# Another order of five engines' work in a cross-attention and six-layer kernel

## The reference

```python
qkv = x @ Wqkv                      # 128 -> 3 * 1024, 16 heads of 64
q = l2norm(q) * qs                  # per head
k = l2norm(k) * ksc
q = q * cos * scale + rotate_half(q) * sin * scale
k = k * cos * inv + rotate_half(k) * sin * inv
sim = einsum(q, k) * QK_SCALE       # windows of 32 queries, 64 keys, band mask
attn = softmax(sim); out = einsum(attn, v)
out @ Wo
...
xn = (x - mu) / sqrt(var + 1e-05) * g + bln
a, gate = split(xn @ W1 + b1)       # 128 -> 2 * 341
a * gelu(gate) @ W2 + b2
```

## Time and profile before

| | |
|---|---|
| median of 3 runs | 1734.22 us (1728.39 to 1739.47) |
| the profiled execution | 1738.27 us, span 1736.5 us |
| mean granted TensorE clock | 0.967 |
| PE busy | 1532.5 us, 88% |
| PEld busy | 1223.3 us, 70% |
| DVE busy | 1360.1 us, 78% |
| ACT busy | 1244.8 us, 72% |
| POOL busy | 1264.0 us, 73% |

### The profile page before, as it was taken

One profiled execution on the slowest core, in us unless ns is written; L12 is line 12 of the kernel. 1 busy time (PEld: TensorE's weight loads), 2 busy tenths in 40 slices (PEclk: granted clock), 3 DMA queues, 4 the chain that ended last, 5 costly groups with the idle time before them and its releaser, 6 DMA issues.

```text
span 1736.5 us, 67874 instructions
## 1 busy us (share of the span) xinstructions
PE 1532.5 (88%) x28560; PEld 1223.3 (70%) x28656; DVE 1360.1 (78%) x2564; ACT 1244.8 (72%) x4601; POOL 1264.0 (73%) x1492
## 2 busy tenths in 40 slices
PE   6589989899998899999889998989999989989985
PEld 5367777677777677777667777767777767777774
DVE  4678888878887977877878787787788787887873
ACT  3267868777877777777777777786776777776773
POOL 2378787777877867867767768787778687887770
PEclk8699999999999999999999999999999999999998
DMA  4012211021211111211111212111211112111011
GB/s 120 1 40 57 57 40 52 27 58 33 67 57 35 45 47 45 67 45 47 33 28 57 67 38 60 33 40 46 57 51 47 47 33 57 27 49 45 27 45 31
DMA packets 50878, 80.62 MB, mean 46 GB/s; under 512 B 8947, under 2 KB 16806, under 8 KB 50574
## 3 DMA queue, kind: packets, MB, share of 16 engines
q1 hardware_dynamic: 50574, 76.28, 15.8%
HBM read 18.62 MB, written 1.05 MB: 11 GB/s over the span
## 4 chain that ended last, share of the span: by engine, by line
PE 63%; ACT 12%; DVE 11%; issue 7%; POOL 7%; DMA 0%; SPq 0%; POOLq 0%; DVEq 0%
PE ps L442 9%; PE ps L389 7%; PE ps L396 7%; ACT pr L650 7%; PE ps L412 6%; PE ps L452 6%; PE ps L391 5%; PE ps L390 5%; PE ps L423 4%; PE ps L483 4%; DVE v L956 2%; ACT sq L613 2%; PE ps L406 2%; POOL t L779 2%; POOL t L798 2%
## 5 line engine op out<-in xcount | busy, mean ns | idle before, releaser
L779 POOL TENSOR_TENSOR t<-t 128x512 f32<-128x512 f32 x384 | 486.2, 1279 | 84.2 <-DVE t L951 83.6
L650 ACT ACTIVATE pr<-ps,nmax 128x64 f32<-128x64 f32 x1536 | 460.6, 353 | 0.9 <-DVE nmax L966 0.9
L798 POOL TENSOR_TENSOR t<-t,rn 128x512 f32<-128x512 f32 x384 | 397.6, 1056 | 7.5
L650 ACT ACTIVATION_READ_ACCUMULATOR pr<-ps,nmax 128x1 f32 x1536 | 376.8, 248 | 0.0
L949 DVE TENSOR_TENSOR t<-ps,rope 128x512 f32<-128x512 f32 x384 | 261.6, 681 | 58.1 <-PE ps L396 37.9
L809 POOL TENSOR_TENSOR pr<-pr,rsum 128x512 f32<-128x512 f32 x192 | 200.8, 1046 | 135.1 <-DVE rsum L973 134.4
L389 PE MATMUL ps<-w_hi,xt_hi 128*128 128x512 f32 x576 | 272.7, 473 | 26.7 <-DVE t L951 10.3
L613 ACT ACTIVATE sq<-ps 128x512 f32<-128x512 f32 x384 | 233.3, 622 | 69.9 <-PE ps L391 63.2
L951 DVE TENSOR_TENSOR t<-ps,rope 128x512 f32<-128x512 f32 x384 | 260.7, 679 | 0.0
L931 DVE TENSOR_REDUCE ss<-sq 128x8 f32<-128x512 f32 x384 | 259.2, 675 | 0.7
L390 PE MATMUL ps<-w_lo,xt_hi 128*128 128x512 f32 x576 | 235.0, 408 | 3.0 <-issue 3.0
(11 more groups left out here) (122 smaller groups left out, 2714.0 us busy)
## 6 DMA issues: line engine op xcount, KB each, us to landing
v_win<-v SPq DMA_DIRECT2D x384, 128.0 KB, 2.3
wqkv<-wqkv_in SPq DMA_DIRECT2D x36, 256.0 KB, 3.9
xsh<-xr SPq DMA_DIRECT2D x24, 224.0 KB, 2.6
wo<-wo_in SPq DMA_DIRECT2D x6, 512.0 KB, 3.8
w<-w_in SPq DMA_DIRECT2D x6, 342.0 KB, 4.6
w<-w_in SPq DMA_DIRECT2D x6, 172.5 KB
x<-x_in SPq DMA_DIRECT2D x4, 256.0 KB, 4.1
out<-x SPq DMA_DIRECT2D x4, 256.0 KB, 2.7
```

Of the source, the lines that this page charges most:

```text
L650: i = A(pr[:, c, odd * SPAN:(odd + 1) * SPAN], ps[:, S_BANK[odd], c * SPAN:(c + 1) * SPAN], ACT.Exp, bias=nmax[:, odd, c:c + 1], accum_out ...
L779: G.tensor_tensor(t1[:, c, :], t1[:, c, :], t2[:, c, :], ALU.add).then_inc(qk_added[c], 1)
L798: G.tensor_tensor(w, w, rn[:, par(u), h2, a, :].unsqueeze(2).broadcast_to([P, 8, E]), ALU.mult).then_inc(done, 1)
```

## The change

The reordering touches every engine's `step(s)`; no computation is added or removed. TensorE's scores now stand between the two transposes of the probabilities, and the values come after projections Q0 and V1 of the following step, so there is other work between both. FFN gates 1 and 2 and value 0 move to the end of the step of gate 0, and `ffn_transpose` moves a step forward. `copy_o` of half 0 moves from VectorE to ScalarE. Twelve entries of the bank tables are set anew, waits are added or dropped as the order needs, the w1 splits come earlier, and `LAST_STEP` is 103. The diff, with its repeated waits on banks cut:

```diff
-    QKV_BANK = [1, 1, 0, 0, 0, 1]
-    TQ_BANK = [5, 4, 4, 5]
+    QKV_BANK = [1, 1, 0, 0, 0, 0]
+    TQ_BANK = [5, 5, 4, 5]
     TP_BANK = [4, 5]
-    GATE_BANK = [0, 1, 0]
-    VALUE_BANK = [1, 0, 1]
+    GATE_BANK = [1, 0, 1]
+    VALUE_BANK = [0, 1, 0]
     O_BANK = [6, 7]
-    Y_BANK, D_BANK, X_BANK, XH_BANK = 6, 7, 6, 5
+    Y_BANK, D_BANK, X_BANK, XH_BANK = 7, 6, 7, 4
-    FIRST_STEP, LAST_STEP = -7, 102
+    FIRST_STEP, LAST_STEP = -7, 103
```

SyncE:

```diff
-                run_layer(s, -4, load_w1, 1)
+                run_layer(s, -5, load_w1, 1)
...
+                run_quad(s, 6, shift_tokens)
                 run(s, 1, shift_v, 1)
-                run_quad(s, 6, shift_tokens)
                 run_layer(s, 2, load_wo, 1)
-                run(s, 0, shift_v, 0)
+                run(s, 1, shift_v, 0)
```

ScalarE, `step(s)` after:

```diff
+                run(s, 1, square, K1)
+                run(s, 1, upper_w, K1)
+                run_quad(s, 9, ffn_gate, 0)
+                run(s, 3, copy_pT, 0)
+                run_input(s, 10, copy_xt)
+                run_quad(s, 9, ffn_gate, 1)
+                run_quad(s, 9, ffn_gate, 2)
+                run(s, 1, guess_norm)
+                run_quad(s, 8, ffn_upper)
+                run(s, 3, copy_pT, 1)
                 run(s, 0, square, Q0)
                 run(s, 0, upper_w, Q0)
+                run(s, 2, exps, 0)
+                run(s, 3, copy_o, 0)
+                run(s, 3, copy_o, 1)
                 run(s, 1, copy_qk, Q0)
+                run(s, 2, exps, 1)
                 run(s, 1, copy_qk, K0)
                 run(s, 0, square, K0)
                 run(s, 0, upper_w, K0)
+                run(s, 1, upper_w, V1)
+                run(s, 1, copy_qk, Q1)
+                run(s, 1, upper_w, V0)
+                run(s, 0, square, Q1)
+                run(s, 0, upper_w, Q1)
+                run(s, 2, exps, 2)
+                run(s, 2, exps, 3)
+                run(s, 1, copy_qk, K1)
```

GpSimd, `step(s)` after:

```diff
+                run(s, 1, normalise_q, 1)
+                run(s, 1, normalise_k, 0)
+                run_quad(s, 7, ffn_power)
+                run(s, 1, rotate, K1)
                 run(s, 1, lower_w, K1)
+                run(s, 1, lower_w, V1)
+                run(s, 1, normalise_k, 1)
+                run(s, 2, normalise_p, 0)
+                run(s, 0, rotate, Q0)
+                run(s, 0, rotate, K0)
+                run(s, 0, lower_w, K0)
+                run(s, 2, normalise_p, 1)
+                run_layer(s, 4, split_w1_gates)
+                run_layer(s, 4, split_w1_values)
+                run(s, 0, rotate, Q1)
+                run(s, 0, refine_norm)
+                run(s, 0, normalise_q, 0)
+                run_quad(s, 6, copy_half)
```

VectorE, a wait in `copy_v` and `step(s)` after:

```diff
             def copy_v(u, odd):
                 dve.wait_ge(qkv_ps[V0 + odd], u + 1)
+                if u >= 2:
+                    dve.wait_ge(o_ps, 4 * (u - 1))
...
+                run(s, 0, sum_squares, Q0)
                 run_quad(s, 7, ffn_stats)
+                run(s, 1, copy_v, 1)
                 run(s, 0, rotary, Q0)
                 run(s, 0, lower_w, Q0)
+                run(s, 1, copy_v, 0)
+                run(s, 2, inverse_sum, 0)
+                run_quad(s, 7, ffn_normalise)
+                run_quad(s, 8, ffn_lower)
+                run(s, 0, rotary, K0)
                 run(s, 0, rotary, Q1)
                 run(s, 0, lower_w, Q1)
+                run_quad(s, 7, ffn_affine)
                 run(s, 0, sum_squares, Q1)
+                run(s, 3, add_residual)
                 run(s, 2, inverse_sum, 1)
+                run(s, 0, sum_squares, K0)
                 run_quad(s, 9, ffn_residual)
                 run(s, 0, sum_squares, K1)
+                run(s, 1, lower_w, V0)
+                run(s, 0, clamp_norm)
+                run(s, 0, rotary, K1)
+                run_quad(s, 8, ffn_gated, 0)
+                run_quad(s, 8, ffn_gated, 1)
                 run_input(s, 9, lower_xt)
+                run_quad(s, 8, ffn_gated, 2)
                 run(s, 1, row_max)
```

182 lines of the change are left out of this document (66 added, 116 removed).

## The result

The changed kernel is slower: 1799.55 us (median of 4 runs, 1791.88 to 1801.93) against 1736.85 of the kernel before beside it, a ratio of 1.036 [1.032, 1.041]. The forecast was 1682 with a range to 1745. The profiled execution took 1800.02 us with a span of 1798.2; TensorE's mean granted clock was 0.958 of full speed (0.967 before).

What follows compares the result with a forecast made beforehand. TensorE was taken as the bound (88% busy, 63% of the chain), with pauses from its instruction stream running dry. Terms -55, -7 and +10 sum to -52, from 1734 to 1682 us; range 1635 to 1745, likeliest case 1640 to 1716.

Steps and rivals of the forecast that it cites:

- Rival D: TensorE's pauses are not its instruction stream and stay wherever small matmuls stand: 1737 us, chance 0.10.
- the term of -55 us: Scores away from values: work between them hides instruction-stream pauses, keeping 15 of 69.9 us; bounds 0 and -70.
- 0 for the step: Plain step: a closed chain through TensorE, ScalarE and VectorE of 13.05 us, against 13.25 before, so no change.
- The FFN term, -7 us: Four steps of an FFN quad: 61.8 us against 62.1 without pauses, 24 quads; bounds -40 and +65.
- The fourth has stats ahead of copy_v and normalise, 4 x 0.48: Fourth step of an FFN quad: normalise ahead of rotary K0 and Q1 delays K1; the step takes 14.65 us.
- 18.0 for that step: Step of gate 0 in an FFN quad: gates, GELUs, values and gated products follow one another, taking 18.0 us.
- half of the serial hand-overs uncovered: Upper bound of the FFN quads' time: 3 us a quad more, +65 us.
- Rival C: Gate steps: gated products ahead of row_max on VectorE delay exponentials and next scores; 3 us a quad, 1754, chance 0.14.
- Rival B: Plain steps: the closed chain takes the gain as late events meet; 0.55 us a step more, 1735, chance 0.16.
- The layer change, +10 us: GpSimd's earlier w1 split waits for value 2, making q 0 1.6 to 2.8 us late in 5 layers; bounds 0, +20.
- Hidden, with no slack: Plain step: copy_v's new wait for values and rotary Q0 behind it cost nothing; K0 needs rotary at 5.05, due 5.0.

Runs made afterwards that it cites:

- experiment 1: Kernel before, with only the values moved behind projection V1 and copy_v waiting for the values two units back: 1744.55 us, 1.0034.
- version 12: Kernel after, with the quad's normalisation in two 128x512 instructions in place of four of 128x128: 1761.14 us, 1.016.
- 5: Kernel after, with the four normalise instructions on ScalarE, using a bias that GpSimd makes: 1770.82 us, 1.022.
- experiment 2: Kernel after, with one of the four normalise instructions, three quarters of the FFN's input left out: 1724.02 us, 0.992.
- experiment 9: Kernel before, with value 2 directly behind value 1 and gated 2 behind gated 1, making that hand-over serial: 1757.81 us, 1.012.
- experiment 3: Kernel after, with the w1 splits back in their old, later steps and w1's load one step later: 1785.9 us, 1.027.
- experiment 13: Kernel after, with normalisation in two large instructions, w1 splits late, clamp_norm on GpSimd and rope_tables two steps later: 1733.98 us, 1.000.
- experiment 4: Kernel after, with VectorE's row_max ahead of the three gated products and of lower_xt: 1798.54 us, 1.035.
- 15: Kernel after, with normalisation in two large instructions, w1 splits late and rope_tables two steps later, clamp_norm staying on VectorE: 1742.36 us, 1.004.
- experiment 16: Kernel after with two-piece normalisation, late w1 splits, clamp on GpSimd, later rope_tables, and copy_pT 1 ahead of guess_norm: 1772.74 us, 1.024.

## Why the prediction was wrong

**What bounds the kernel, and the pauses.** That the pauses belong to TensorE's instruction stream at dense small matmuls held: separated, they went from 69.9 to 2.9 us, and experiment 1 cut them by 33 us in the old order as well. Behind the cross-attention 60 of 63 spacings between pauses of over 0.6 us are within 6 of a multiple of 253 recorded instructions in the kernel before, and all 24 in the kernel after, most of them now at the scores. The queue still moves 226 packets. Rival D is out: the pauses did not stay where the small matmuls are. What failed is the step from a wait that ends to time that is won, the term of -55 us. I set it against a bound of 0 that I tied to another cause, took the pause off whole, and charged nothing for the values' later place, behind which `copy_o`, the copies of the transposes and `copy_v` queue. Experiment 1 shows both together at 6 us slower, with 41 us of new waits for ScalarE and VectorE; it does not divide them between work that was late anyway and work that the move made late. In the changed kernel the plain step is 1.0 us shorter, where I had predicted 0 for the step and 0.6 for the pause (55/96). That part of the sum was there, and was spent again on other steps of the quad.

**The FFN term, -7 us: the other step that failed.** "The fourth has stats ahead of copy_v and normalise, 4 x 0.48". The duration was taken from the place that the instruction had in the old order. In the new place it is 1.06 in the mean (4.4 us in the quad that I showed), since VectorE's instructions wait for GpSimd's 1.04 to 1.30 us products there. The prediction did not lay the two engines side by side at the new place. The Trainium skill has the rule, in "SBUF — State Buffer", section Who interferes with whom: VectorE and GpSimd share a port pair, held for a whole instruction, so that the later one stands until the first has finished; this concerns a VectorE instruction with two SBUF inputs (against a GpSimd one that reads SBUF) or in one of its two-port modes. For VectorE the traces agree: 1.24 for four beside small work and 4.45 beside large in the kernel after; 0.17 for the clamp beside an idle GpSimd, 1.14 at 544.49 in the kernel after, beside a rotation from 544.32; no lengthening of products that read PSUM, nor on ScalarE (491 ns). That GpSimd stands behind VectorE, no row here shows. Priced by experiment: the held part is -38 us by 12 and -29 by 5, and each of these may still pay something of its own, more elements or 23.2 us of ScalarE's waiting for the bias. 75 us (experiment 2) is the upper end, with the work itself in it. The clock is in these prices: of the second intervals 12 of 24 were below full clock in the kernel after, 3 in version 12, and 1 in that of experiment 2.

**The hand-overs of gates and values.** I had 18.0 for that step and "half of the serial hand-overs uncovered" as the bound of +65. The fourth interval grew by 3.1 us, the size of that bound; whether by that mechanism is another question. The chain that ended last shows the stretch (start, us, what):

```profile
557.88 1.36 PE ps L412 x88
559.25 1.66 issue
...
561.80 0.24 PE ps L462
...
562.53 0.70 ACT gate L668
...
563.27 0.49 PE ps L468
...
564.34 0.76 DVE hT L1027
...
565.15 0.49 PE ps L468
...
566.14 0.76 DVE hT L1027
...
567.04 0.47 PE ps L389
...
567.97 1.53 PE ps L440 x96
```

Two things lie on it. A pause of 1.66 us, now in the scores, with nothing to hide it. And gate 1, GELU, value 0, gated, value 2, gated, V1, one behind the other, with 0.04 to 0.14 us of "issue" at each. TensorE has gate 2, value 1 and Q0 to do meanwhile: its waits for gated products are 9.7 us in the whole kernel, 6.8 before. What it waits for in the fourth interval, in us a quad and against next to nothing before unless said, is `copy_v` 0.5, the pauses in the scores 0.5 (0.07 before), GpSimd's product for the transposes 0.4, the rotary product at a gate chunk 0.3, gated products 0.4 (0.3). With the 1.1 us more of busy time, in which the lower clock is, these make up nearly all of the 3.1. So the serial hand-overs of gates and values, which I had made the bound, are not shown to be what the interval pays for; experiment 9 prices such a link at 22 us where nothing covers it. The layer change has 0.87 a quad of it, by experiment 3, with which the fourth intervals below full clock went from 8 to 2. With four edits (13) the interval is 21.03, still 0.9 over before.

**Rival C** gave 1754 and the direction, with 0.14. Its price for the step, 3 us, was met, which is in good part luck: its mechanism, the maxima behind the gated products, is seen at 0.7 us a quad in experiment 4, which that run loses again at `lower_xt`, and it accounts for neither the second interval nor the 75 us of normalise. **Rival B**, 1735, is in the end what stands where the added costs are taken out: experiment 13 gives 1734, and in its list waits for rotary and ScalarE's copies lead. The wait that B names is there in the kernel after, 58.3 us for the rotary product. But its place is less the plain interval (0.5 us of it), which is at 13.60 in version 13, than the second (1.2 us).

**The layer change, +10 us,** was right: 14 by experiment 3, within its bounds of 0 to 20, and the GpSimd waits, 18.5 and 7.1 us, stand where they were put. "Hidden, with no slack" for `copy_v` and rotary was too kind: the waits of L389 for `copy_v` rose from 2.5 to 17.3 us, and those for rotary from 10.3 to 58.3, of which experiment 2 takes 25 away.

**The sum, as the experiments give it.** The pauses 0 net of what their move costs (experiment 1: +6); normalise about +38; w1 +14; clamp and rope tables about +13, of which the clamp 8 by experiments 13 and 15. That is 65 against 63 measured. The 13 is what experiment 13 leaves after the other two (1761 - 1734 - 14), so the sum closing is no test of its parts; it also leaves out what is left of the longer fourth interval, and sets the 1.0 us that the plain step gained against it. That the four edits together bring the kernel back to 1734 is measured.

**Open:** why the start and the end grew by 5 us each (of the latter 0.4 by the two last additions `x<-x,xr`), what the pauses' end is worth without the values' later place, and what exactly fills the 1.6 us that the second interval of version 13 is longer than that of before, where third and plain are shorter.

## What to carry to other kernels

A wait that vanishes is worth only what lies behind it, less what the move that removes it makes late: list who is due within the same microsecond, and who waits for the work that moves, before it is counted. An experiment on one move needs the same look: two of those above made a new wait that hid what they were to show. A moved VectorE instruction from SBUF to SBUF takes the duration of its new neighbourhood: lay GpSimd's timeline beside the new place, and put such work beside its idle or short stretches, in few large instructions, or on ScalarE. A cheap step at the head of a line through a busy engine should not be put behind anything: 0.6 us of copy ahead of the guessed norm cost 39 us (experiment 16).

## What the runs showed of the hardware

VectorE and GpSimd alternate one instruction for one: four instructions of 128x128 took 4.45 us beside four of GpSimd, 1.24 us beside short ones, and the one-input form was held alike (median 1080 against 1126 ns). A held instruction ended 0.15 us behind GpSimd's (86 of 87 in the kernel after). GpSimd showed no loss in this: its rotation took 1.29 and 1.30 us in the contested stretch, 1.27 us at 540.51 in the same trace, beside products that read PSUM; the medians of its two commonest products are 1277 and 1042 ns, 1278 and 1043 before.

TensorE's pauses follow the small matmuls: with the values moved away from the scores they came down from 69.9 us to 2.9 at the values, while the scores' own rose from 11.8 to 25.3 us, up to 2.2 in one piece. They come at multiples of some 253 recorded instructions (60 of 63 spacings before, all 24 after). Not every wait for "issue" is one of them: in experiment 4 it was 21.9 us at the values, and 16.7 of that had another spacing, once a quad, and ended with VectorE's `lower_xt`.

TensorE's granted clock was 0.66 and 0.62 in the 5 and 4.5 us behind two long stands of 1.80 and 2.59 us, and 1.00 between them. Less waiting brought it back: its mean was 0.958 in the kernel after and 0.978 in version 13.
